# First edge group: the merged rows' statistics ahead of the third sort's counts, attention, W1 and the sort some steps later

## The reference, cut

```python
xn = _layernorm(x, axis=-1)
agg = segment_sum(edge_weight[:, None] * xn[dst], src, N_NODES)
gnn = agg @ W + b                                # edge part
Q, K = elu(xn @ Wq) + 1, elu(xn @ Wk) + 1        # dense part, 8 heads
msg = (Q @ (K^T v)) * Z                          # linear attention
msg = layernorm(msg @ Wm, g1, b1)
h = relu(concat([xn, msg]) @ W1) @ W2
mix = xn + layernorm(h, g2, b2)
x = x + gnn + mix
x = x + experts(layernorm(x))                    # 16 experts, top 2
```

## Time and profile before

| | |
|---|---|
| median of 3 runs | 1204.18 us (1203.69 to 1205.10) |
| profiled execution | 1204.72 us, span 1202.6 |
| busy share of the span | TensorE 88%, VectorE 66%, GpSimd 52%, ScalarE 42% |
| first group | from 107.50 (first tile) to 175.78 (`prefix(3)`) |
| a later group | 48.53 (group 2's to group 3's list pick, 236.10 to 284.63) |
| chain by engine | TensorE 63%, VectorE 22%, issue 7% |

### The profile page before, as it was taken

The page is one execution under the profiler, slowest core; times in us unless marked ns, Lnnn a source line. Parts: engine busy times, 40 slices in busy tenths (PEclk is TensorE's granted clock), DMA queues, the critical chain, the costliest instruction groups (busy, mean ns, idle before and its releaser), DMA issues.

```text
span 1202.6 us, 20286 instructions
## 1 busy us (share of the span) xinstructions
PE 1057.6 (88%) x6272; PEld 919.3 (76%) x6272; DVE 788.1 (66%) x2010; ACT 505.4 (42%) x1162; POOL 623.4 (52%) x626
## 2 busy tenths in 40 slices
PE   6897779899998999999989897729999999999980
PEld 5785667787877877878778776229999999999980
DVE  7987688889889898898897768762222222222226
ACT  4444745675675855757657564410101101010100
POOL 6957566767667676676676640011333333333320
PEclk9999899999999999999999999859999999999995
DMA  7314222223223232232332320366999999999948
GB/s 214 106 49 124 70 75 76 86 83 97 83 84 97 80 93 83 81 96 84 89 92 81 92 71 1 108 218 207 337 331 338 320 342 331 334 335 325 333 157 319
DMA packets 113480, 196.03 MB, mean 163 GB/s; under 512 B 13505, under 2 KB 61439, under 8 KB 113407
## 3 DMA queue, kind: packets, MB, share of 16 engines
q1 hardware_dynamic: 84073, 120.62, 29.9%
q0 software_dynamic: 26112, 71.34, 19.0%
q10 hardware_dynamic: 3222, 3.20, 0.8%
HBM read 177.12 MB, written 17.99 MB: 162 GB/s over the span
## 4 chain that ended last, share of the span: by engine, by line
PE 63%; DVE 22%; issue 7%; DVEq 4%; ACT 2%; DMA 2%; SPq 0%; POOL 0%; ACTq 0%; POOLq 0%
PE psum L1100 19%; PE psum L998 11%; PE psum L1110 9%; PE psum L889 7%; DVE agg L1389 6%; PE psum L898 4%; PE psum L1010 3%; DVE agg L1383 3%; PE psum L750 2%; PE psum L846 2%; DVE agg L1867 1%; DVE count L1169 1%; PE psum L796 1%; PE psum L1088 1%; PE psum L778 1%
## 5 line engine op out<-in xcount | busy, mean ns | idle before, releaser
L692 POOL DMA_INDIRECT arena<-y_rows,gather_i x416 | 448.0, 1077 | 203.7 <-PE psum L1010 74.0
L998 PE MATMUL psum<-arena,hot 128*128 128x256 f32 x832 | 217.0, 393 | 20.3 <-DVE agg L1383 13.8
L1383 DVE TENSOR_TENSOR agg<-psum,agg 128x256 f32 x416 | 174.1, 419 | 46.5 <-DVE agg L1383 27.1
L998 PEld LDWEIGHTS psum<-arena,hot 128*128 128x128 f32 x832 | 153.1, 194 | 48.5 <-issue 29.2
L1100 PEld LDWEIGHTS psum<-arena 128*128 128x128 f32 x1536 | 181.4, 194 | 5.0 <-issue 2.6
L1100 PE MATMUL psum<-arena 128*128 128x128 f32 x1536 | 181.9, 277 | 2.0 <-DVE arena L1824 2.0
L515 ACT ACTIVATE arena<-arena,listed 128x256 f32<-128x256 f32 x416 | 172.8, 496 | 17.1 <-DMA arena<-y_rows,gather_i 17.0
L1831 DVE TENSOR_TENSOR arena<-psum,arena 128x512 f32<-128x512 f32 x64 | 44.3, 692 | 205.0 <-PE psum L1100 205.0
L708 POOL DMA_INDIRECT chosen_rows<-arena,back_at x64 | 63.2, 988 | 220.1 <-DVE arena L1838 215.4
L626 ACT ACTIVATE arena<-psum 128x512 f32<-128x512 f32 x64 | 38.2, 597 | 328.1 <-PE psum L1100 328.1
L1010 PE MATMUL psum<-arena,first_use 128*128 x624 | 149.3, 383 | 3.3 <-DVE agg L1389 3.1
(11 more groups left out here) (222 smaller groups left out, 1507.4 us busy)
## 6 DMA issues: line engine op xcount, KB each, us to landing
arena<-in_L_ffn_w_dram SPq DMA_DIRECT2D x144, 512.0 KB, 5.7
xnT<-in_L_ffn_w_dram SPq DMA_DIRECT2D x48, 512.0 KB
arena<-y_rows,gather_i POOLq DMA_INDIRECT x416, 2.8
arena<-chosen_rows SPq DMA_DIRECT2D x4, 1280.0 KB, 9.7
y_rows<-w ACTq DMA_DIRECT2D x6, 512.0 KB, 2.9
agg<-in_x_dram SPq DMA_DIRECT2D x4, 640.0 KB, 6.7
n_rows<-arena SPq DMA_DIRECT2D x4, 640.0 KB
out_dram<-agg SPq DMA_DIRECT2D x4, 640.0 KB
```

What stands on the lines that cost most here:

```text
L692: pool.indirect_dma_start(rows[h][:, t, :], None, y_rows, bass.IndirectOffsetOnAxis(ap=gather_i[h][:, t:t + 1], axis=0)).then_inc(gathered ...
L998: pe.matmul(bank_of(g, t // 2)[:, (t % 2) * C:(t % 2 + 1) * C], hot[:, (g * GT + t) % HOTS, :], rows[h][:, t, :], start=True, stop=True).t ...
L1383: dve.tensor_tensor(own, bank_of(g, t // 2)[:, (t % 2) * C:(t % 2 + 1) * C], own, ALU.add).then_inc(evicted, 1)
```

## The change

In group 0 alone, some steps of TensorE's and VectorE's lists move. On TensorE: attention from step 3 to 5, the first turning from 9 to 11, the merge from 12 to 14, the second turning from 19 to 21, the first three quarters of W1 from 21, 22, 23 to 23, 24, 25, `prefix(2)` from 20 to 26, the second query from 25 to 27, the last quarter from 29 to 30, `down` from 34, 35 to 35, 36, and three of the four reorderings by one to three steps. On VectorE: the sums from 4 to 6, the messages from 5, 6 to 7, 8, the statistics of the merged rows stay at step 13 but without the scan ahead of them, the moments go from 14 to 15, the root from 16 to 17; the marks of the third sort go from 11 to 15, its counts from 13 to 19, its later parts by four to seven steps, its records by up to six; the statistics of the down product go from 36 to 37. Three `dve.drain()` fall away.

```diff
--- before.py
+++ after.py
@@ -901,38 +901,38 @@
                     last.then_inc(d_down, 1)
 
             def beside_first(step):
-                if step == 3:
-                    attend(0)
                 if step == 4:
                     turn_list(1)
-                if step == 9:
+                if step == 5:
+                    attend(0)
+                if step == 11:
                     turn_tok(0, d_msg, d_msgT)
-                if step == 12:
-                    merge(0)
                 if step == 13:
                     pick_list(1)
-                if step == 19:
+                if step == 14:
+                    merge(0)
+                if step == 21:
                     turn_tok(0, d_n1, d_n1T)
-                if step == 20:
+                if step == 23:
+                    hidden(0, 0)
+                if step == 24:
+                    hidden(0, 2)
+                if step == 25:
+                    hidden(0, 1)
+                if step == 26:
                     prefix(2)
-                if step == 21:
-                    hidden(0, 0)
-                if step == 22:
-                    hidden(0, 2)
-                if step == 23:
-                    hidden(0, 1)
-                if step == 25:
+                if step == 27:
                     query(1)
-                if step == 29:
+                if step == 30:
                     hidden(0, 3)
-                if step == 34:
+                if step == 35:
                     down(0, 0)
-                if step == 35:
+                if step == 36:
                     down(0, 1)
                 if step == 49:
                     attend(1)
-                if step in (33, 40, 46, 54):
-                    reorder(2, (33, 40, 46, 54).index(step))
+                if step in (36, 42, 47, 54):
+                    reorder(2, (36, 42, 47, 54).index(step))
 
             def beside(g, step):
                 sorts, more = g + 2 < NG, g + 1 < NG
@@ -1468,49 +1468,45 @@
                 if step == 1:
                     keys_and_values()
                     query_elu(0)
-                if step == 4:
+                if step == 6:
                     message_sums(0)
                     dve.drain()
                     message_shares(0)
                     dve.drain()
-                if step in (5, 6):
-                    message(0, step - 5)
-                if step == 11:
+                if step in (7, 8):
+                    message(0, step - 7)
+                if step == 13:
+                    pair_stats(0, 0, d_merged, 5)
+                    keep_picked(1)
+                if step == 15:
+                    pair_moments(0, 0)
                     mark_bins(2)
-                    keep_picked(1)
-                if step == 13:
-                    dve.drain()
+                if step == 17:
+                    first_root(0)
+                if step == 19:
                     count_marks(2)
-                    pair_stats(0, 0, d_merged, 5)
-                if step == 14:
-                    dve.drain()
-                    pair_moments(0, 0)
-                if step == 16:
-                    first_root(0)
-                if step == 17:
+                if step == 22:
                     add_prefix(2)
-                if step == 18:
-                    dve.drain()
+                if step == 24:
                     mask_places(2)
-                if step == 19:
+                if step == 25:
                     dve.drain()
                     sum_places(2)
-                if step == 20:
+                if step == 26:
                     dve.drain()
                     split_places(2)
                     dve.drain()
                     keep_places(2)
-                if step in (21, 27, 31, 37):
+                if step in (27, 31, 35, 40):
                     dve.drain()
-                    mark_tiles(2, (21, 27, 31, 37).index(step))
-                if step in (24, 30, 36, 43):
+                    mark_tiles(2, (27, 31, 35, 40).index(step))
+                if step in (29, 33, 38, 43):
                     dve.drain()
-                    make_record(2, (24, 30, 36, 43).index(step))
-                if step in (26, 29, 38, 44):
-                    mark_slots(2, (26, 29, 38, 44).index(step))
-                if step == 36:
+                    make_record(2, (29, 33, 38, 43).index(step))
+                if step in (28, 32, 39, 44):
+                    mark_slots(2, (28, 32, 39, 44).index(step))
+                if step == 37:
                     pair_stats(1, 0, d_down, 4)
-                if step == 37:
                     dve.drain()
                     pair_moments(1, 0)
                 if step == 39:
```

## The result

The changed kernel takes **1210.53 us** (median of 5, 1209.71 to 1211.49) against 1203.69 (median of 5, 1201.98 to 1205.10) for the kernel before on the same chip: a ratio of **1.0059**, 95% interval 1.0046 to 1.0072, 5.5 to 8.7 us longer. The forecast was 1208.3 in a range of 1202.0 to 1211.0: right in its sign and in its main mechanism, 2.2 us short in its size, 0.5 inside the range's upper end. It was added to a median before of 1204.18; against the 1203.69 measured beside it the kernel lost 6.84, where 4.1 was forecast.

A forecast was written before the change was run, and what follows sets the result against it. Bound: group 0's chain of waits, three engines taking turns. Later pair 0.8 to 2.3, half level 1.7, tail 1.45: 4.0 to 5.4; less group 1's recovery, 3.5 to 4.9, taken 4.1: 1208.3 us, range 1202.0 to 1211.0.

The forecast's parts named there:

- The message 1.3 later: VectorE's message in group 0, complete at 119.8 where it was at 118.5: 1.3 us later.
- First scaling 1.0 earlier or 0.5 later: ScalarE's first scaling, from 128.89 to 127.9 with TensorE at full level, or 129.4 at half level.
- Tile 20 as the longest wait: TensorE stalls over 4 us at tile 20 for ScalarE's scaling, its longest wait of the group; start 130.5 or 132.1.
- `n1_turned` 1.6 to 3.1 later: ScalarE's copy of the turned rows, behind tiles 20, 21 and the transposes: 133.1 or 134.6, not 131.5.
- ScalarE's work unchanged to the query: ScalarE still needs 12.6 us after the turned rows' copy, so the second query starts at 146.3 to 147.8, not 144.66.
- The wait for the prefix about 7: VectorE waits 7 us, not 4.45, for prefix sums behind W1's three parts; cost nothing, not what ends last.
- Half level behind the query, taken 1.7 (0 to 3.4): TensorE's half clock level after its wait for the second query, costing nothing to 3.4 us; 1.7 taken.
- The tail 1.45 longer: VectorE's work after the pair of steps 36 and 37 gains down statistics (0.65) and third record (0.8).
- Group 1 takes back at most 0.51: Group 1 recovers at most the 0.51 us that VectorE waited there for the merge; the rest is shifted whole.
- level holds: Rival, chance 0.24: TensorE's clock stays full at the first turning and ahead of the query; 1.7 us longer, 1205.9.
- Faster: Rival, chance 0.10: tiles 20 and 21 do not hold the transposes, the earlier first scaling carries through; 2.6 shorter, 1201.6.
- Slower still: Rival, chance 0.11: the half level lasts through merge, turning and query, twice the 1.7; 1210.5.

The follow-up runs named there:

- e9: Changed kernel plus unread matmuls in two TensorE waits: 9 calls ahead of tile 20, 8 ahead of the second query; 1208.98 us.
- e1: Changed kernel with the second turning alone put back at step 19, ahead of tiles 20 and 21; 1207.15 us.
- e4: Changed kernel plus 16 matmul calls, results never read, ahead of the second query; 1212.87 us.
- e5: Changed kernel plus 8 matmul calls, results never read, ahead of the second query; 1207.77 us.
- e2: Changed kernel with ScalarE's scaling of tiles 20 to 23 moved ahead of std and the first scaling; 1205.91 us.
- e12: Changed kernel with attention, first turning, merge and VectorE's sums and messages back at their old steps; 1208.39 us.
- e10: The changed kernel's VectorE list with the whole TensorE list of the kernel before; 1210.21 us.
- e8: Kernel before with the third sort's counts behind the root and ScalarE's scaling of tiles 20 to 27 ahead of std and first scaling; 1199.93 us.
- e3: Changed kernel with the third sort's prefix sums at TensorE's step 22 instead of 26, ahead of W1's first three parts; 1208.28 us.
- e11: Kernel before with only ScalarE's scaling of tiles 20 to 27 moved ahead of std and the first scaling; 1203.66 us.

## Why the prediction was right, and where its size was off

By its own steps, from the first tile of the group (107.50 before, 106.87 after):

- *The message 1.3 later*: 12.29 for 11.00, 1.29. Right.
- *First scaling 1.0 earlier or 0.5 later*: 21.95 for 21.39, 0.56 later; the half-level case. The merge's lateness ate the scan's 1.83, as worked out. Right.
- *Tile 20 as the longest wait*: 4.32 on ScalarE's scaling, begun at 24.61; the half-level case said 132.1, which is 24.6. Right.
- *`n1_turned` 1.6 to 3.1 later*: 3.7. Here the first piece is missing. I took the two tiles at 0.86 each, already the half-level pace (twice the 0.43 of a tile at full level), but the transposes at 0.76, nearer to their 0.66 at full level (e9's line in the last section) than to the 1.06 that they took at half level, behind a stall that I said would bring it. From tile 20 to `n1_turned` it is 2.97 where the sum had 2.48, 0.49 more.
- *ScalarE's work unchanged to the query*: 3.67 later there, all of it handed on. Right.
- *The wait for the prefix about 7*: 6.89, and it ended nothing in after, as said. But "its own work alone would end the group 1 us later" was wrong: with the turning put back, VectorE ran without a wait to an end 2.36 later (e1). It did not matter for the forecast, only for what an edit could win back.
- *Half level behind the query, taken 1.7 (0 to 3.4)*: **the term that was mis-sized**. It measured 3.0 (e4, e5). I chose the smaller stretch because the work behind the query is unbroken; the trace shows 15 matmuls in 6 us at 0.52 in spite of that. In the path, query to pair was 15.55 where the sum had 12.58 + 1.7, 1.27 more.
- *The tail 1.45 longer*: 19.25 for 17.68, 1.57. Right.
- *Group 1 takes back at most 0.51*: nothing. VectorE's wait there shrank by 0.21 (0.30 at 189.95 for 0.51), but group 2 begins as late as group 1 did.

The upper end of the sum was 5.4. The misses on it are 0.58 at `n1_turned`, 1.27 behind the query and 0.12 in the tail: 7.37, and the group is 7.35 longer. The 1.27 and most of the 0.58 are one thing twice: what TensorE's half level costs in work that follows a wait. That the forecast lay below its own upper sum was a choice, too: it took the middle of two cases, and the half-level one came.

Of the rivals, "level holds" happened in one trace (e9) with about its price, so its working was sound and its condition did not hold. Its argument that the 0.82 stall cost no level does not stand: that stall lies inside the stretch of 0.57. "Faster" is excluded for this form: ScalarE's order does hold tile 20, and where that was undone (e2) VectorE's tail still left a loss. "Slower still", 1210.5, is the number that came out: it took 3.4 for the half level where 3.0 was measured behind the query. But 1208.8 and 1.7 more is 1210.5 on the profiled execution's scale; on the median's, as the forecast, it is 1210.0.

The drains: eviction to next instruction is 0.34 without one (126.43 to 126.77) where the earlier trace rows has 0.50 with it (126.75 to 127.25), 0.16 each as priced. The Trainium skill, VectorE: DVE Perf Modes, section The DRAIN you can't avoid, says that the pipeline is flushed after every operation, but that a next operation that is not held starts earlier; the 0.34, less than the eviction's own 0.42, agrees with the latter. The sum counted nothing for the drains, and three are 0.5 us at most, beside a loss of 7.35.

How the 7.35 divides is not a plain sum, since the edits overlap: e1 alone returns 5.0, e12 2.7, e5's level 3.0. Shown are the turning behind tile 20 with its half level as the larger part (e1 and e2, which undo it, and e12, where the first scaling was early and `n1_turned` still late) and the tail of about 1.5 as the part that no edit returned: it is 19.25 us, within 0.01, in the trace of after and of every edit made to it. The split of the rest is not settled, and e10, which loses as much at the median without that turning, is not explained by one trace.

## What to carry to other kernels

When a step is moved behind another on one engine, look at what that other step itself waits for on a third engine: the transposes were not slow, they stood behind a tile that waited for ScalarE. Then cost all the work after each new long TensorE wait, the short pieces too, at half-level durations from the trace, and take the longer stretch; in this case the half level did not follow every wait. To win an early start of a chain, free its next link too (e8 moved the scaling along with the statistics) before moving anything else.

## What the runs showed of the hardware

The wait that precedes the half level did not fix whether it came. In after it followed waits of 1.99 and 1.97 us (0.72 over 112 to 118 and over 118 to 124), while in e3 a wait of 2.00 ahead of the query left the level full. Two kernels that are the same up to this point waited the same 3.65 us for the message; TensorE's timeline and the stretch of e5, then TensorE's timeline of e9 (whose stretch stands above; L1426 and L1429 are L1424 moved down by the added lines):

```profile
119.73 1.12 PE L870 MATMUL psum<-ident,wv 128*128 128x128 f32 x4 [3.65 <-DVE wv L1426]
```

```profile
118.00:124.00 6.00, 4.27 (x12) 3.26 (x13) 3.70 (x9) 2.19 (x5) 4.48 (x6) 0.57 0.30 91
```

```profile
120.01 0.66 PE L870 MATMUL psum<-ident,wv 128*128 128x128 f32 x4 [3.65 <-DVE wv L1429]
```

In e5 the transposes took 1.12 us and the stretch ran at a mean of 0.57; in e9 they took 0.66 and it ran at 1.00. The Trainium skill, TensorE: Matmul & The Clock Gate, section Part 1, has the clock fall when the engine idles; the stretches shown here agree, each of those below full level stands behind a wait; but the same wait went both ways. This goes with the spread of one kernel's executions (e5: 1204.75 to 1210.32), though only one execution of each has a trace, so the connection is argued and not shown. The mean granted clock on record for each whole execution points the same way in e5 (0.959 for the shortest, 0.954 for the longest) and in e1 (0.960 and 0.955), but in e2 and e11 it does not follow the time. The other surprise: unread matmuls ahead of the query shortened the kernel by 2.8 us at the median.
